# One projection unit in every head step of an attention and spline-FFN kernel: v0 in head 10, v3 in the next batch's head 1, later output, query and key units

## The chip, the cores and the metric

One core of a Trainium2 chip. The metric is the device time of one execution in microseconds, and the before figure is the median of three runs. A profiled execution of the same kernel gives the trace. The engines are named as in the trace: PE (TensorE, the matmuls), PEld (its weight loads), DVE (VectorE), ACT (ScalarE), POOL (GpSimd), and SP (SyncE, which only issues DMAs here).

## What is computed

Four batches of 512 tokens with 512 features, all in float32. After a layer norm, the result is `x + attention(xn) + ffn(xn)`.

```
xn = layernorm(x)
q, k, v = xn@Wq+bq, xn@Wk+bk, xn@Wv+bv          # 16 heads of 32
scores = q k^T / sqrt(32) + slope[h] * distance, causal
ctx = softmax(scores) @ v
attention = ctx @ Wo + bo
ffn: gate, up, down weights (2048 x 512) are Catmull-Rom splines through few control points;
     silu(xn@gate^T) * (xn@up^T) @ down
out = x + attention + ffn
```

To keep float32 precision on fast matmuls, an operand is split into a high part and a low part (high = the value rounded, low = value minus high), and a product is three matmuls: high x high, high x low, low x high.

## The kernel before

The attention of all four batches runs first, then the FFN. The change touches the attention alone. It is a software pipeline of 64 head steps (4 batches x 16 heads), written out by hand and the same on every engine. There is one `step(b, s, ...)` function per engine, and each engine runs its instructions strictly in the order written. What crosses engines goes by semaphores.

In head step s the stages belong to different heads. PE makes the scores of head s (four row tiles of 128 queries, `scores`, L624), transposes the probabilities of head s-2 (`turn_probs`, L638), and multiplies by the values for head s-3 (`weigh_values`, L655 and L658). DVE adds the bias and takes the row maximum of head s (`bias_and_max`, L830, one call for tiles 0 and 1 and one for tiles 2 and 3), copies half of what PE turned (`take_turned`, L839), and normalizes head s-3 (`normalize`, L848, L849, L856). ACT takes exponentials (L1049), rounds them to the high half (`probs_high`, L1057, which waits for PE's last turn of the step, so that it runs at the start of the next step), and copies the remaining turned tile (L1064). POOL makes the low half of the probabilities of head s-1 (`probs_low`, L1160).

There are two score banks. Tile 2 of a head can be scored only when DVE has read tile 0. And `bias_and_max` of head s waits in its first instruction until `probs_low` of head s-2 is done, because the probabilities have two buffers:

```
if (later(b) or s >= 2) and tiles[0] == 0:
    dve.wait_ge(lo_ready, H * b + s - 1)
```

Between these stages the projections are spread over the heads. A unit is 12 matmuls of 512 columns (L583, L584, L585): ("q", c) and ("k", c) make four heads' queries or keys, ("v", t) the values of one tile of 128 tokens, ("o", t) one tile of the output projection of the batch before. `UNITS` says which unit stands in which head step, `TURNS` where a context chunk ("c") or a tile of the next batch's normalized x ("x") is transposed on PE (L668, L573), and `place` says to which batch an entry belongs. The first unit of a step is cut up and put between the attention stages (pieces 0 and 1 ahead of the scores of tiles 2 and 3, piece 2 between the turns, piece 3 behind the values); another unit of the step stands at the end of it. Before, heads 9 and 10 hold no unit, and heads 11 and 13 hold two.

A q or k unit goes on through ACT (`qk_high`, L1023 and L1030), POOL (`qk_low`, L1155), and three DMAs by SP into `q_stack` or `k_stack`. A v unit goes through DVE (`v_take`, L806), and then twice, for heads 0 to 7 and 8 to 15, through ACT (`v_high`, L1042) and DVE (`v_split`, L816, L818, L820, which `SPLITS` places at the end of DVE's step). An x tile goes through statistics (`norm_stats`, L777 to L784), `inverse_std` on POOL (L1148), `norm_apply` on DVE (L789), the transposes, `x_high` on ACT (L1011) and `x_low` on DVE (L798). The units and turns share three PSUM banks in turn, each of which is freed by the low-half operation three entries before. `project_qk` of q0 waits until `x_low` of the last x tile is done.

SP's queue holds the stack DMAs, the store of each sum tile (`store_sum`), the load of the next x tile into the same place (`room_for_x`), and in the last batch the loads for the FFN. Of these, `load_basis` brings the moment basis, for which PE waits in head 12 of the last batch (L695).

Of the kernel before, what the change touches and what calls it, by code (L numbers as in the profile page):

```python
# [239 lines left out]
def build_kernel(nc, x, wq, wk, wv, wo, bq, bk, bv, bo, cpts, c_factor, c_bases, c_mask, c_dist, c_ident, c_scale,  # L240
# [11 lines left out]
    with ExitStack() as outer:  # L252
# [155 lines left out]
        def _(sp):  # L408
# [6 lines left out]
UNITS = {0: [("k", 1)], 1: [("q", 2)], 2: [("o", 0)], 3: [("k", 2)], 4: [("o", 1)], 5: [("o", 2)], 6: [("o", 3)],  # L415
         7: [("q", 3)], 8: [("k", 3)], 11: [("v", 0), ("q", 0)], 12: [("k", 0)], 13: [("v", 1), ("q", 1)],
         14: [("v", 2)], 15: [("v", 3)]}
# [5 lines left out]
SPLITS = {13: [(0, 0)], 14: [(0, 1)], 1: [(0, 2)], 2: [(0, 3)], 4: [(1, 0)], 5: [(1, 1)], 6: [(1, 2)], 7: [(1, 3)]}  # L423
# [23 lines left out]
PJ_FIRST = [("x", t) for t in range(QT)] + [("q", 0), ("k", 0)] + [("v", t) for t in range(QT)] + [("q", 1)] + (  # L447
# [50 lines left out]
def attention(nc, ctx, sems, psum, w_room, v_room, xt_room, stored, lay_out, weights, bq, bk, bv,  # L498
# [65 lines left out]
    def attention_tensor(pe):  # L564
# [144 lines left out]
        def step(b, s, carry):  # L709
# [4 lines left out]
            early, rest = ([], units) if s == 3 else (units[:1], units[1:])  # L714
# [36 lines left out]
        for t in range(QT):  # L751
            project_v(0, t)
# [20 lines left out]
    def attention_vector(dve):  # L773
        def norm_stats(b, tiles):
            for t in tiles:
                dve.wait_ge(x_ld[t], 16 * b + 16)
                dve.bn_stats(stats[:, t, :], x_in[:, t, :]).then_inc(ln_stats, 1)  # L777
# [95 lines left out]
        def step(b, s, carry, carried):  # L873
# [41 lines left out]
            for of, (kind, n) in turns if s not in (3, 11) else []:  # L915
# [29 lines left out]
        norm_stats(0, (0, 1))  # L945
        norm_stats(0, (2, 3))
# [20 lines left out]
        for t in range(QT):  # L967
# [12 lines left out]
        for s in range(HALF, H + 3):  # L980
            step(B - 1, s, False, False)
# [23 lines left out]
    def attention_scalar(act):  # L1005
# [771 lines left out]
```

## Time and profile before

| | |
|---|---|
| time before, median of 3 runs (lowest to highest) | 768.01 us (766.4 to 770.3) |
| the profiled execution's own time | 770.39 us |
| its span, first to last instruction | 768.6 us |
| mean granted TensorE clock, share of full | 0.961 |
| PE busy | 682.4 us (89%) |
| DVE, ACT, POOL busy | 461.0, 445.1, 330.8 us |

A time in the trace counts from the span's start. Head 0 of batch 0 starts at 38.75 us. One round of 16 head steps (head 9 of batch 1 to head 8 of batch 2) goes from 196.63 to 302.56 us. The last heads end near 464 us, and the rest is the FFN. A row of the timeline gives start and length in microseconds, then the engine and the line; in square brackets stands how long the engine was idle before it and what ended that. In a row of the windows, (x56) counts instructions; the three numbers at the end are the granted clock as a share of full speed, the share of the DMA engines, and GB/s.

### The profile page before, as it was taken

What the parts mean: (1) busy time and instruction counts of PE and PEld (TensorE: products, weight loads), DVE (VectorE), ACT (ScalarE), POOL (GpSimd) and SP (SyncE); (2) the same over time, 40 slices, a digit from 0 to 9 for tenths busy, and PEclk for the clock granted to TensorE, in tenths of its full rate; (3) what the DMA queues carried; (4) which work ended last, traced back from release to release, by engine and by line L of the source; (5) the groups of instructions that cost most, each with busy time, mean ns of one, the idle gap of its engine ahead of it and who ended that gap; (6) DMA issues with size and microseconds to landing.
All of it is one profiled execution on the core that took longest, in us unless ns stands there. A gap on an engine that the chain in (4) does not pass through costs nothing.

```text
span 768.6 us, 13687 instructions
## 1 busy us (share of the span) xinstructions
PE 682.4 (89%) x4884; PEld 545.7 (71%) x4884; DVE 461.0 (60%) x1290; ACT 445.1 (58%) x705; POOL 330.8 (43%) x191
## 2 busy tenths in 40 slices
PE   4878789989799898899897777788979999999997
PEld 3766567877578786788776665566758887887885
DVE  6277976879867879768798696665323213223122
ACT  4388758777777977787879764444423332232331
POOL 1565535454545644454546430222225236235334
PEclk9989989999899999899999999999989999999999
DMA  7887386377675374862946938857157475344001
GB/s 244 160 187 126 42 238 117 63 142 172 88 200 80 47 123 103 194 104 43 209 81 96 372 108 270 258 144 275 55 150 246 139 231 173 90 126 128 34 1 55
DMA packets 53067, 109.75 MB, mean 143 GB/s; under 512 B 6408, under 2 KB 6664, under 8 KB 51464
## 3 DMA queue, kind: packets, MB, share of 16 engines
q1 hardware_dynamic: 51416, 106.46, 56.6%
q10 hardware_dynamic: 1584, 2.43, 1.2%
q8 instruction: 39, 0.64, 0.4%
q14 instruction: 28, 0.23, 0.1%
HBM read 59.32 MB, written 25.17 MB: 110 GB/s over the span
## 4 chain that ended last, share of the span: by engine, by line
PE 40%; DVE 5%; issue 4%; POOL 3%; ACT 3%; DMA 2%; ACTq 1%; SPq 0%; POOLq 0%; DVEq 0%
PE bank L1486 6%; PE bank L1488 6%; PE bank L1487 6%; PE bank L1473 3%; PE bank L1474 3%; PE bank L583 3%; PE bank L638 2%; PE bank L585 2%; PE bank L584 2%; POOL resid L1640 2%; DMA bm_early<-bases_scratch 2%; PE bank L624 2%; DVE w_new L1584 1%; ACTq L365 1%; PE bank L655 1%
## 5 line engine op out<-in xcount | busy, mean ns | idle before, releaser
L1160 POOL TENSOR_TENSOR work<-work 128x1280 f16<-128x1280 f32 x64 | 171.3, 2676 | 176.4 <-ACT work L1057 176.4
L1632 POOL TENSOR_TENSOR in_lo<-inner,in_hi 128x512 fp32r<-128x512 f32 x64 | 84.9, 1328 | 201.1 <-ACT in_hi L1550 201.1
L830 DVE CUSTOM_DVE_ANT_0 work<-bank,dist 128x128 f32<-128x128 f32 (+3 forms) x256 | 115.4, 487 | 72.0 <-PE bank L624 48.4
L1049 ACT ACTIVATE work<-work,neg_max 128x128 f32<-128x128 f32 (+3 forms) x256 | 130.0, 561 | 13.8 <-DVE neg_max L830 13.5
L1550 ACT CAST in_hi<-inner 128x512 fp32r<-128x512 f32 x64 | 39.7, 621 | 147.3 <-PE bank L1488 141.3
L1596 DVE TENSOR_TENSOR inner<-bank,silu 128x512 f32<-128x512 f32 x64 | 44.1, 689 | 132.2 <-ACT silu L1544 125.4
L1057 ACT CAST work<-work 128x1280 f16<-128x1280 f32 x64 | 80.6, 1259 | 61.1 <-PE bank L638 60.9
L638 PE MATMUL bank<-ident,work 128*128 128x128 f16 x1280 | 107.7, 229 | 9.1 <-DVE work L839 7.1
L638 PEld LDWEIGHTS bank<-ident,work 128*128 128x128 f16 x1280 | 77.5, 102 | 45.4 <-issue 32.3
L1486 PE MATMUL bank<-w_room,in_hi 128*128 128x512 f32 x256 | 101.6, 397 | 0.4 <-POOL in_lo L1632 0.4
L1487 PE MATMUL bank<-w_room,in_hi 128*128 128x512 f32 x256 | 101.0, 394 | 0.0
L1488 PE MATMUL bank<-w_room,in_lo 128*128 128x512 f32 x256 | 100.9, 394 | 0.0
L624 PE MATMUL bank<-k_stack,q_stack 96*128 96x256 f32 (+2 forms) x256 | 78.1, 380 | 20.3 <-DVE neg_max L830 18.2
L839 DVE COPY work<-bank 128x256 f16<-128x256 f16 (+2 forms) x192 | 75.6, 418 | 6.4 <-PE bank L638 6.2
L624 PEld LDWEIGHTS bank<-k_stack,q_stack 96*128 96x128 f32 x256 | 46.9, 201 | 35.8 <-DVE neg_max L830 29.6
L655 PE MATMUL bank<-v_parts,work 128*128 128x98 bf16 x640 | 68.9, 215 | 2.5 <-issue 2.0
L658 PE MATMUL bank<-v_parts,work 128*128 128x66 bf16 x640 | 66.3, 199 | 0.0
L1064 ACT COPY work<-bank 128x1024 f16<-128x1024 f16 x64 | 64.3, 1005 | 2.5 <-PE bank L638 2.5
L1473 PE MATMUL bank<-z,wgu_hi 128*128 128x512 f32 x128 | 52.1, 407 | 9.2 <-issue 4.8
L655 PEld LDWEIGHTS bank<-v_parts,work 128*128 128x128 f16 x640 | 54.4, 102 | 6.5 <-issue 2.8
L1486 PEld LDWEIGHTS bank<-w_room,in_hi 128*128 128x128 f32 x256 | 49.2, 192 | 11.9 <-POOL in_lo L1632 1.5
L583 PE MATMUL bank<-xt_room,w_room 128*128 128x512 f32 x128 | 55.9, 437 | 1.9 <-DVE xt_room L798 1.9
(100 smaller groups left out, 1298.7 us busy)
## 6 DMA issues: line engine op xcount, KB each, us to landing
q_stack<-parts SPq DMA_DIRECT2D x48, 256.0 KB, 5.7
k_stack<-parts SPq DMA_DIRECT2D x48, 256.0 KB, 6.1
z<-xt_scratch SPq DMA_DIRECT2D x128, 88.0 KB
x_in<-x SPq DMA_DIRECT2D x32, 256.0 KB, 4.0
xt_scratch<-xt_room SPq DMA_DIRECT2D x8, 1024.0 KB, 7.3
xt_room<-xt_scratch SPq DMA_DIRECT2D x6, 1024.0 KB, 10.2
factor<-c_basis SPq DMA_DIRECT2D x5, 1024.0 KB, 9.2
taps<-windows SPq DMA_DIRECT2D x5, 1024.0 KB, 11.1
```

Of the source, the lines that this page charges most:

```text
L583: pe.matmul(bank[:, :], l_hi, r_hi, start=(k == 0), stop=False)
L624: pe.matmul(score_bank[i % 2][:, 0:n], q_stack[:, c % 2, h, i * P:(i + 1) * P], k_stack[:, c % 2, h, 0:n], start=True, stop=True).then_inc ...
L638: mm = pe.transpose(pt_bank[i % 2][:, (part * n + k) * P:(part * n + k + 1) * P], probs16[:, s % 2, part, OFF[i] + k * P:OFF[i] + (k + 1) ...
L655: pe.matmul(bank[:, i * VALUES:(i + 1) * VALUES], probs_t[:, s % 2, at:at + P], v_parts[:, k, s, :], start=(k == 0), stop=False)
L830: dve.tensor_tensor_reduce(probs[:, s % 2, OFF[i]:OFF[i] + n], score_bank[i % 2][:, 0:n], dist[:, S - n:S], -slope(s), 3.4e38, ALU.add, AL ...
L1049: e = act.activation(tile, tile, ACT.Exp, bias=neg_max[:, s % 2, i:i + 1], scale=-1.0)
L1057: act.copy(probs16[:, s % 2, 0, :], probs[:, s % 2, :]).then_inc(hi_ready, 1)
L1160: pool.tensor_tensor(probs16[:, s % 2, 1, :], probs[:, s % 2, :], probs16[:, s % 2, 0, :], ALU.subtract).then_inc(lo_ready, 1)
L1486: pe.matmul(sum_bank[i][:, :], hi, wd_hi[:, g, :], start=(g == 0), stop=False)
L1487: pe.matmul(sum_bank[i][:, :], hi, wd_lo[:, g, :], start=False, stop=False)
L1488: mm = pe.matmul(sum_bank[i][:, :], lo, wd_hi[:, g, :], start=False, stop=(g == NG - 1))
L1632: pool.tensor_tensor(in_lo[k % 2][:, :], inner[:, k % 2, :], in_hi[:, k % 2, :].bitcast(F32), ALU.subtract).then_inc(il_ready, 1)
```

## The change

Each head step now holds exactly one unit. v0 stands in head 10 and v3 in head 1 of the batch that it belongs to (in batch 0 too, where it left the stretch ahead of head 0). q2 and k2 move from heads 1 and 3 to 3 and 4, o1 to o3 from 4, 5, 6 to 5, 6, 7, q3 and k3 from 7 and 8 to 8 and 9, q1 from 13 to 14, v2 from 14 to 15. In head 10 the unit stands at the end of PE's step. On DVE, the low halves of x tiles 0 and 1 stand between the two calls of `bias_and_max` in head 10, `v_take` of v0 stands there in head 11 ahead of the low halves of x tiles 2 and 3, and the statistics of tile 3 with the aggregation of tiles 2 and 3 move from head 8 to head 9. On POOL, `inverse_std` of the second pair moves to step 10, and in every step `qk_low` now stands ahead of `probs_low`. On ACT, `v_high` of v3 stands between the exponentials and `probs_high` of head 2. On SP, each x tile's load is asked for behind the next tile's store, and `load_basis` stands ahead of the stacking of q3 and k3 of the last batch.

```diff
-UNITS = {0: [("k", 1)], 1: [("q", 2)], 2: [("o", 0)], 3: [("k", 2)], 4: [("o", 1)], 5: [("o", 2)], 6: [("o", 3)],
-         7: [("q", 3)], 8: [("k", 3)], 11: [("v", 0), ("q", 0)], 12: [("k", 0)], 13: [("v", 1), ("q", 1)],
-         14: [("v", 2)], 15: [("v", 3)]}
+UNITS = {0: [("k", 1)], 1: [("v", 3)], 2: [("o", 0)], 3: [("q", 2)], 4: [("k", 2)], 5: [("o", 1)], 6: [("o", 2)],
+         7: [("o", 3)], 8: [("q", 3)], 9: [("k", 3)], 10: [("v", 0)], 11: [("q", 0)], 12: [("k", 0)], 13: [("v", 1)],
+         14: [("q", 1)], 15: [("v", 2)]}
-SPLITS = {13: [(0, 0)], 14: [(0, 1)], 1: [(0, 2)], 2: [(0, 3)], 4: [(1, 0)], 5: [(1, 1)], 6: [(1, 2)], 7: [(1, 3)]}
+SPLITS = {13: [(0, 0)], 15: [(0, 1)], 1: [(0, 2)], 2: [(0, 3)], 4: [(1, 0)], 5: [(1, 1)], 6: [(1, 2)], 7: [(1, 3)]}
...
@@ PE, step
-            early, rest = ([], units) if s == 3 else (units[:1], units[1:])
+            early, rest = ([], units) if s in (3, 10) else (units[:1], units[1:])
...
@@ DVE, step
-                if kind == "v" and n > 0:
+                if kind == "v":
                     v_take(of, n)
...
-            if s == 11:
+            if s in (10, 11):
                 for of, (_, n) in turns:
                     x_low(of, n)
...
             if s == HALF - 1 and b < B - 1:
-                norm_stats(b + 1, (0, 1))
+                tile_stats(b + 1, 0)
+                tile_stats(b + 1, 1)
+                pair_stats(b + 1, (0, 1))
             if carry and s == HALF:
-                norm_stats(b + 1, (2, 3))
-            if carry and s == 11:
-                v_take(b + 1, 0)
+                tile_stats(b + 1, 2)
+            if carry and s == HALF + 1:
+                tile_stats(b + 1, 3)
+                pair_stats(b + 1, (2, 3))
...
@@ ACT, step
                 exponentials(b, s)
+                if s == 2:
+                    v_high(b, 0, 3)
                 probs_high(b, s)
...
@@ POOL, step
-            if carry and s in (8, 9):
-                inverse_std(b + 1, s - 8)
-            if halved:
-                probs_low(*halved)
-
+            if carry and s == 8:
+                inverse_std(b + 1, 0)
+            if carry and s == 10:
+                inverse_std(b + 1, 1)
             if s < H and (s or later(b)):
                 for key in active(UNITS, (s - 1) % H, carried):
                     if key[0] in "qk":
                         qk_low(b + place(key, s - 1), *key)
+            if halved:
+                probs_low(*halved)
...
@@ SP
-            store_sum(b - 1, 1)
-            store_sum(b - 1, 2)
-            room_for_x(b, 0)
-            room_for_x(b, 1)
-            store_sum(b - 1, 3)
-            room_for_x(b, 2)
-            room_for_x(b, 3)
+            for q in range(1, QT):
+                store_sum(b - 1, q)
+                room_for_x(b, q - 1)
+            room_for_x(b, QT - 1)
+        load_basis(sp)
         stack(B - 1, 3)
 
         sp.wait_ge(pj_full, pj_total(("k", KC - 1), B - 1))
         load_chunk(sp, 1)
-        load_basis(sp)
```

## Rows read from the trace of the kernel before

**Rows 1.** The page: span; each engine's busy time, share of span, instructions.
```profile
span 768.6 us, 13687 instructions
PE 682.4 (89%) x4884; PEld 545.7 (71%) x4884; DVE 461.0 (60%) x1290; ACT 445.1 (58%) x705; POOL 330.8 (43%) x191
```
**Rows 2.** Windows, a head each (9 to 13, 2, 8): busy, granted clock, DMA.
```profile
196.63:205.96 9.33, 6.01 (x56) 5.16 (x54) 7.58 (x23) 7.77 (x11) 5.72 (x4) 0.72 0.71 108
205.96:212.86 6.90, 4.88 (x54) 4.01 (x53) 5.64 (x18) 5.47 (x9) 2.63 (x2) 0.88 1.03 160
212.86:221.70 8.84, 8.84 (x76) 7.12 (x74) 5.76 (x18) 5.20 (x9) 3.03 (x2) 1.00 0.86 294
221.70:227.29 5.59, 5.59 (x59) 4.45 (x58) 3.49 (x14) 3.80 (x7) 2.33 (x2) 1.00 0.35 70
227.29:235.75 8.46, 8.46 (x73) 6.79 (x70) 6.08 (x19) 7.61 (x11) 5.11 (x3) 1.00 0.67 93
...
258.49:264.65 6.16, 5.62 (x61) 4.44 (x59) 5.41 (x20) 5.98 (x11) 3.87 (x2) 1.00 0.88 123
...
295.63:302.56 6.93, 6.04 (x60) 4.46 (x58) 6.26 (x22) 5.70 (x9) 4.76 (x3) 1.00 0.13 38
sum 105.93, PE 97.54 PEld 78.17 DVE 84.20 ACT 82.47 POOL 53.79; mean PE 6.10 PEld 4.89 DVE 5.26 ACT 5.15 POOL 3.36
```
**Rows 3.** Timeline in head 2, PE and VectorE: start, length (us), line.
```profile
258.49 0.48 PE L624 MATMUL bank<-k_stack,q_stack 96*128 96x256 f32 x2
...
260.06 0.28 DVE L830 CUSTOM_DVE_ANT_0 work<-bank,dist 128x128 f32<-128x128 f32 x1
...
261.18 0.48 PE L583 MATMUL bank<-w_room,ctx_t 128*128 128x512 f32 x1
```
**Rows 4.** Timeline of ScalarE in head 13.
```profile
227.57 1.26 ACT L1057 CAST work<-work 128x1280 f16<-128x1280 f32 x1 [1.44 <-PE bank L638]
...
229.65 0.69 ACT L1023 ACTIVATE qk_full<-bank,b_qk 128x512 f32<-128x512 f32 x1
230.22 0.69 ACT L1030 ACTIVATE parts<-bank,b_qk 128x512 fp32r<-128x512 f32 x1
```
**Rows 5.** Timeline of GpSimd in head 13.
```profile
228.91 2.63 POOL L1160 TENSOR_TENSOR work<-work 128x1280 f16<-128x1280 f32 x1 [4.56 <-ACT work L1057]
231.50 1.28 POOL L1155 TENSOR_TENSOR parts<-qk_full,parts 128x512 fp32r<-128x512 f32 x1
```
**Rows 6.** Timeline of VectorE at the end of head 13.
```profile
232.20 0.73 DVE L856 TENSOR_TENSOR ctx_sb<-ctx_tmp,inv_sum 128x128 f32<-128x128 f32 x1
232.86 0.55 DVE L839 COPY work<-bank 128x768 f16<-128x768 f16 x1
```
**Rows 7.** Timeline in head 9 of batch 0, VectorE and GpSimd.
```profile
95.47 3.33 DVE L789 TENSOR_SCALAR x_in<-x_in,meanvar,rstd 128x512 f32<-128x512 f32 x2
...
95.91 2.61 POOL L1160 TENSOR_TENSOR work<-work 128x1280 f16<-128x1280 f32 x1 [0.99 <-ACT work L1057]
```
**Rows 8.** Timeline of VectorE in head 8: a value split, then the bias.
```profile
297.24 0.42 DVE L816 TENSOR_TENSOR v_room<-v_room,v_parts 128x256 f32<-128x256 f32 x1
...
298.36 0.28 DVE L830 CUSTOM_DVE_ANT_0 work<-bank,dist 128x128 f32<-128x128 f32 x1
```
**Rows 9.** Timeline in head 9 of batch 1, VectorE and PE.
```profile
202.52 0.29 DVE L856 TENSOR_TENSOR ctx_sb<-ctx_tmp,inv_sum 128x128 f32<-128x128 f32 x1
...
204.37 1.94 PE L573 MATMUL bank<-ident,x_in 128*128 128x128 f32 x8 [1.01 <-DVE x_in L789]
```
**Rows 10.** Timeline of VectorE in head 11 of batch 1.
```profile
213.36 0.29 DVE L830 CUSTOM_DVE_ANT_0 work<-bank,dist 128x128 f32<-128x128 f32 x1 [0.37 <-issue]
...
213.92 1.28 DVE L798 TENSOR_TENSOR xt_room<-bank,xt_room 128x512 fp32r<-128x512 f32 x2
```
**Rows 11.** Timeline in head 12 of the last batch, PE.
```profile
431.53 0.47 PE L695 MATMUL bank<-xt_room,bm_early 128*128 128x512 f32 x1 [3.42 <-DMA bm_early<-bases_scratch]
```
**Rows 12.** Timeline at the start of head 0, batch 0, PE.
```profile
38.75 0.48 PE L624 MATMUL bank<-k_stack,q_stack 96*128 96x256 f32 x2 [1.13 <-DMA k_stack<-parts]
```

More of the change, by code:

```diff
@@ L444 @@
 STACK = 16 * ROLES
-PJ_FIRST = [("x", t) for t in range(QT)] + [("q", 0), ("k", 0)] + [("v", t) for t in range(QT)] + [("q", 1)] + (
+PJ_FIRST = [("x", t) for t in range(QT)] + [("q", 0), ("k", 0)] + [("v", t) for t in range(3)] + [("q", 1)] + (
     steps_keys(range(HALF), before=False))
@@ L455 @@
 MOMENTS = {12: 0, 13: 1, 14: 2}
-PJ_LAST = [("k", 3), ("c", 1), ("m", 0), ("m", 1), ("m", 2), ("c", 2), ("o", 0), ("o", 1), ("c", 3), ("o", 2), ("o", 3)]
-PJ_LAST_ENDS = [("k", 3), ("c", 1), ("m", 0), ("m", 1), ("m", 2), ("c", 2), ("c", 3)] + [("o", t) for t in range(QT)]
-CARRIED = [("k", 3)] + [("c", c) for c in range(1, KC)] + [("o", t) for t in range(QT)] + [
+PJ_LAST = [("q", 3), ("k", 3), ("c", 1), ("m", 0), ("m", 1), ("m", 2), ("c", 2), ("o", 0), ("o", 1), ("c", 3), ("o", 2), ("o", 3)]
+PJ_LAST_ENDS = [("q", 3), ("k", 3), ("c", 1), ("m", 0), ("m", 1), ("m", 2), ("c", 2), ("c", 3)] + [("o", t) for t in range(QT)]
+CARRIED = [("q", 3), ("k", 3)] + [("c", c) for c in range(1, KC)] + [("o", t) for t in range(QT)] + [
     ("m", m) for m in range(3)]
@@ L750, in attention_tensor @@
         project_qk(0, "k", 0)
-        for t in range(QT):
+        for t in range(3):
             project_v(0, t)
@@ L773, in attention_vector, with tile_stats, pair_stats @@
     def attention_vector(dve):
[L774 to L777, printed above, removed]
+        def tile_stats(b, t):
+            dve.wait_ge(x_ld[t], 16 * b + 16)
+            dve.bn_stats(stats[:, t, :], x_in[:, t, :]).then_inc(ln_stats, 1)
+        def pair_stats(b, tiles):
             dve.wait_ge(ln_stats, QT * b + tiles[-1] + 1)
@@ L914, in step @@
                 norm_apply(b + 1, 3)
-            for of, (kind, n) in turns if s not in (3, 11) else []:
+            for of, (kind, n) in turns if s not in (3, 10, 11) else []:
                 (x_low if kind == "x" else ctx_low)(of, n)
@@ L944, in attention_vector @@
         dve.memset(minus_half[:], -0.5).then_inc(small_set, 1)
-        norm_stats(0, (0, 1))
-        norm_stats(0, (2, 3))
+        for n in range(2):
+            for t in (2 * n, 2 * n + 1):
+                tile_stats(0, t)
+            pair_stats(0, (2 * n, 2 * n + 1))
         for t in range(QT):
@@ L966, in attention_vector @@
         dve.wait_ge(dist_ld, 16)
-        for t in range(QT):
+        for t in range(3):
             v_take(0, t)
@@ L974, in attention_vector @@
             for s in range(HALF, H):
-                step(b - 1, s, True, s > HALF)
+                step(b - 1, s, True, s > HALF or b > 1)
             for s in range(HALF):
@@ L980, in attention_vector @@
         for s in range(HALF, H + 3):
-            step(B - 1, s, False, False)
+            step(B - 1, s, False, s == HALF)
             if s - 1 in MOMENTS:
@@ L1085, in step @@
             for half, t in SPLITS.get((s + 1) % H, []) if s < H else []:
-                if s >= HALF - 1 and carry and half == 0:
-                    v_high(b + 1, half, t)
-                elif s < HALF - 1:
+                if s >= HALF - 1 and half == 0:
+                    if carry:
+                        v_high(b + 1, half, t)
+                elif s < HALF - 1 and (half, t) != (0, 3):
                     v_high(b, half, t)
```

## Prediction

> **What bounds the kernel now.** I read the page first: PE is busy 89% of the span, the others 43% to 60% [rows 1]. Then I cut one round of 16 head steps into its heads with the windows view. A head with one unit takes 5.59 us and PE is busy for all of it; a head with two takes 8.84 (11, with a context turn) or 8.46 (13). So a unit is worth 8.46 - 5.59 = 2.87 us of PE, and a context turn 8.84 - 8.46 = 0.38. PE idles in few heads: 9 (9.33 us long, 6.01 busy), 10 (6.90, 4.88), 8 (6.93, 6.04) and 2 (6.16, 5.62) [rows 2]. The granted clock is 1.00 nearly everywhere and 0.72 and 0.88 in heads 9 and 10, so part of their time is at the lower level, 1.2 GHz. The round is 105.93 us with 97.54 of PE. The plan's promise is plain: move the two second units into the two empty heads.
>
> Last I read the timeline for the slack of the other engines, counting from a head's start. The first bias of a head has a due time. In head 2 it starts at 260.06, +1.57, and PE resumes its unit at 261.18, 1.12 later [rows 3]; the head is 6.16 - 5.59 = 0.57 long over, of which the context turn is 0.38, so 0.19 is from lateness. In head 8 it starts at 298.36, +2.73 [rows 8], and the head is 1.34 over [rows 2]. Both give the same due time, about +1.39: each microsecond of a later bias is one of the head.
>
> **The change, part by part.**
>
> *POOL's new order.* In head 13 (start 227.29), which handles the k unit of head 12, ACT makes `probs_high` from +0.28 and the unit's high half until 230.91, +3.62 [rows 4]. POOL makes `probs_low` at +1.62 (2.63 us) and `qk_low` after it (1.28 us) [rows 5]. With `qk_low` first, in-order POOL waits for +3.62, so `qk_low` ends at +4.90 and `probs_low` at +7.53, not +4.25. Behind it waits the first bias of the next head (the `lo_ready` wait): 7.53 - 5.59 = +1.94, which is 0.55 late. That is the least price of a q or k unit in a full-length step.
>
> *The collision on top.* DVE's L856 takes 0.29 us alone [rows 9] but 0.73 when it starts at +4.91 in `qk_low`'s span (+4.21 to +5.49); it ends at +5.64, 0.15 after POOL [rows 5, 6]. In batch 0 the two L789 took 3.33 us together where the first `probs_low` of 2.61 lay over them [rows 7]; so POOL's long operation holds them too. In the new order `probs_low` lies at +4.90 to +7.53, just over L856 and the value split that follows L839 (L839 ends at 233.41, +6.12 [rows 6]; the split takes 298.36 - 297.24 = 1.12 [rows 8] and reads two SBUF tensors like L856). The bounds for a split behind a k unit: it isn't held, the bias is due to `probs_low` alone (0.55 late), or it starts only when POOL ends, and the bias starts at 7.53 + 1.12 = 8.65, +3.06 in the next head, 1.67 late (about 1.8 if L856 gets in first and pushes POOL back by part of its 0.29). If the head itself is already d late, L856 falls inside `probs_low` and waits as well: 7.53 + 0.29 + 0.55 + 1.12 = 9.49, which is 2.51 - d late. I take the held case, since L856 is nearest in kind.
>
> The Trainium skill ("SBUF — State Buffer", section "SBUF: two separate sides") says that VectorE and GpSimd take their common port pair as an exclusive lock for the whole instruction, whoever starts first. That L856 ends 0.15 after POOL's operation agrees. By that rule the close race at +4.90 against +4.91 goes to whoever is first; were it always POOL, heads 0 and 2 would pay some 0.7 more each, 4 us over three rounds.
>
> Price for a round: head 13 (q0; no split in 12) 0.85, which is 0.55 plus L856's 0.3; head 14 (k0; 13 already late) 2.51 - 0.85 = 1.66; head 0 (q1; head 15 has a context turn, 0.38 of slack) 1.4; head 2 (k1) 1.8, less the 0.19 it pays today, plus 0.3 for `v_take` of v3 in DVE's chain to the context turn, 1.9; head 5 (q2 comes at the end of 3, so POOL is free early) 0.4; head 6 (k2) 2.51 - 0.4 = 2.1. Sum 8.3 us.
>
> *Heads 9 to 11.* Head 9: POOL holds `probs_low` until about +7.8, so `norm_apply` of the first tile waits; two of these at 0.5 and the last x turn at 0.6 give 9.4 (before 9.33, for other reasons). Head 10: the bias waits for the moved statistics (+0.6), the low halves of x0 and x1 in front of the second bias call take 1.28 [rows 10] more, DVE's copies reach PE's last turns at about +3.9, and v0 stands whole behind them: 3.9 + 0.8 + 2.87 + two x turns of 0.4 = 8.4 (before 6.90). Head 11: q0 is now the early unit and waits for the last `x_low`. DVE starts the bias at 213.36, +0.50, and would be ready for other work at 213.92, +1.06 [rows 10]; `v_take` now goes first (0.6, like one of the two L798), then 1.28: +2.95. The unit before started near +0.55, so head 11 is 5.59 + 2.4 + 0.38 = 8.4 (before 8.84). Together 26.2 against 25.07: +1.1. If ACT's extra k unit ahead of `x_high` binds, heads 9 and 10 trade the wait but the sum stays (7.6 + 9.4).
>
> *Gains.* Head 13 gives back one unit, -2.87. Head 3 is 0.2 longer, from the bias behind a split that starts later. A round: -2.87 + 8.3 + 1.1 + 0.2 = +6.7 us.
>
> *The rest.* Three such rounds: +20.1. In the first one the 3.33 us pair [rows 7] probably falls elsewhere: about -3. Ahead of head 0, v3's leaving gains nothing, because PE waits there for a stack DMA that it doesn't touch [rows 12]. Heads 0 to 7 of batch 0 keep four units, but pay two held splits: 2 x 1.7 = +3.4. In the last batch `load_basis` early takes away the wait of 3.42 us [rows 11]; against it k3 goes to head 9, which had none (up to 2.87), and POOL's order costs 0.55 or more once: about 0. SP's other new order puts the load of x tile 2 behind the store of tile 3, which I cost at nothing, because the stores come a head later anyway and the statistics of tile 3 moved by a head; without that cover DVE's statistics in head 7 or 8 wait, at most some 3 us in one batch. Sum: 20.1 - 3 + 3.4 + 0 = +20.5.
>
> The profiled execution has a span of 768.6 and a time of 770.39 us, 2.4 above the median. Its sum would be 789 (span). On the median: 768.0 + 20.5 = 788.5, so **788.5 us**.
>
> **Rivals.**
>
> *(1) POOL's operation doesn't hold the split; only `lo_ready` binds.* For it: splits have hardly lain under `probs_low` so far. Against: L856 and L789 are held. Price a round: heads 13, 2 and 6 pay 0.55, head 0 0.2, `v_take` 0.3, and head 9 shrinks to 7.6 with head 10 at 9.4: 25.3 - 25.07 = +0.2. Sum: 2.15 + 0.2 + 0.2 - 2.87 = -0.3. With +1 for batch 0: about 769.
>
> *(2) The other side: POOL's lateness costs nothing.* If ACT reaches the k and q units some half microsecond earlier than in rows 4 (its exponentials have slack where PE is late), `probs_low` ends by +6.98 = 5.59 + 1.39 and nothing waits: it decides from there. Then a round is -2.87 + 0.2 + 0.2 = -2.5, three are -7.4, and the 3.42 of the last batch comes as well: 757.
>
> *(3) The empty heads fill up entirely.* x's chain hides behind PE, heads 9 to 11 are 6.4 + 6.4 + 6.0 = 18.8 instead of 25.07: another -6.3 a round, 740. Against: q0's wait for `x_low` is in the code, and DVE's rows give +2.95.
>
> *(4) As my forecast, but the clock falls more often.* The new waits of 1.4 to 2.4 us stand in six heads. The granted clock was 0.72 in head 9, where PE was busy 6.01 of 9.33 us [rows 2]. One more low stretch a round with a unit in it costs up to 2.87: 797.
>
> **How the numbers follow.** Forecast 0.52, rival 1 0.18, rival 2 0.14, rival 3 0.04, rival 4 0.12. The forecast's own range is 780 to 796 (each of six prices by a third, the race for 4 us). The range of 758 to 800 leaves out rival 3, the lower half of 2 and the upper part of 4, 0.2 or a little less. A difference within 0.5% (3.8 us) is about what a measurement of this kernel can't tell from none. Slower by more: forecast, 4, and a little of 1, 0.66. Within: most of 1, 0.12. Faster: 2, 3 and the rest of 1, 0.22.
>
> **What the profile after would show.** Heads 2, 6, 14 and 0 longer than 7 us, with L830 preceded by L816 to L820 that start as L1160 ends, and L1155 ahead of L1160. Head 13 near 6.5, not 5.6. In head 11 an idle PE of about 2 us ended by DVE L798. Head 10 over 8 us. No wait on `bm_early`. The prediction is wrong if the first bias in the heads after a q or k unit still starts by +1.4, or if L816 runs at 0.41 us inside L1160.

## The result and the profile after

The changed kernel takes 846.0 us in the median of four runs (843.5 to 847.47), against 768.18 us (766.4 to 770.3) for the kernel before beside it. The ratio is 1.1003, with a 95% interval of 1.0966 to 1.104. The forecast of 788.5 us had the sign, and its range of 758 to 800 missed the size: the loss is 78 us and not 20. The profiled execution took 846.91 us.

The page of the changed kernel, its span and the busy time of each engine:

```profile
span 845.1 us, 13687 instructions
PE 709.4 (84%) x4884; PEld 560.9 (66%) x4884; DVE 529.5 (63%) x1290; ACT 447.3 (53%) x705; POOL 331.3 (39%) x191
```

The instruction counts are those of before [rows 1]. PE is busy 27 us longer with the same matmuls. Most of that is the clock: an estimate from the means of 0.936 and 0.961 over the two spans, at half speed where it is low, gives 24 us. DVE is busy 68.5 us longer with the same instructions, which is waiting inside an instruction: 43 us of it are in the three instructions of the value split, 18 in L857 (L856 before), and 4 in `norm_apply`. ACT and POOL have hardly changed. Where the time lies, by windows of the changed kernel: heads 0 to 8 of batch 0, and the first two of the three rounds of 16 heads. The table has the other stretches too.

```profile
38.40:99.67 61.27, 45.21 (x361) 36.38 (x361) 48.39 (x141) 39.64 (x63) 25.77 (x12) 0.79 0.50 96
99.67:225.61 125.94, 104.18 (x932) 80.98 (x930) 102.92 (x279) 83.10 (x128) 54.38 (x26) 0.93 0.53 116
225.61:354.90 129.29, 106.35 (x933) 82.38 (x930) 105.87 (x279) 83.02 (x128) 54.05 (x26) 0.92 0.48 90
```

| stretch, us | before | after | difference | forecast |
|---|---|---|---|---|
| heads 0 to 8, batch 0 | 48.91 | 61.27 | +12.4 | +3.4 |
| round 1 | 108.97 | 125.94 | +17.0 | +3.7 |
| round 2 | 105.93 | 129.29 | +23.4 | +6.7 |
| round 3 | 106.49 | 129.46 | +23.0 | +6.7 |
| last half batch | 41.95 | 45.28 | +3.3 | 0 |
| FFN and the stretch ahead of head 0 | 356.4 | 353.9 | -2.5 | 0 |

In round 2 PE is idle for 129.29 - 106.35 = 22.9 us, before for 105.93 - 97.54 = 8.4 [rows 2]. So 14.5 us of the 23.4 are idle time, and 106.35 - 97.54 = 8.8 are the same matmuls taking longer. About 7 of these 8.8 are the clock, by an estimate from the means: 129.29 us at 0.92 hold about 21 us of the low level (twice 0.08 of the time), heads 9 and 10 of before [rows 2] about 7, and each such microsecond costs half of one. The rest shows at full clock too: head 13 has 6.02 us of PE at 1.00. The same view for heads of that round (11, 13 and 14 of batch 1; 0, 2 and 6 of batch 2), and first for head 0 of the round before:

```profile
155.82:165.11 9.29, 6.05 (x60) 4.46 (x58) 9.01 (x18) 4.79 (x7) 4.55 (x2) 1.00 0.60 86
...
244.34:254.43 10.09, 7.72 (x64) 5.86 (x61) 5.72 (x17) 2.85 (x6) 0.00 (x0) 0.83 0.87 304
...
260.03:267.12 7.09, 6.02 (x60) 4.45 (x58) 6.64 (x16) 5.58 (x10) 5.16 (x3) 1.00 0.93 137
267.12:277.34 10.22, 7.64 (x61) 5.60 (x58) 8.45 (x20) 4.36 (x6) 3.10 (x2) 0.83 0.51 61
...
283.34:294.19 10.85, 7.61 (x59) 5.73 (x58) 9.09 (x18) 4.79 (x7) 4.56 (x2) 0.84 0.53 74
...
299.81:310.67 10.86, 7.33 (x61) 5.68 (x59) 9.79 (x20) 4.96 (x9) 4.84 (x2) 0.84 0.53 73
...
330.37:341.36 10.99, 7.60 (x60) 5.53 (x58) 9.24 (x20) 4.66 (x7) 4.24 (x2) 0.84 0.67 119
```

Four heads carry most of it: 14, 0, 2 and 6, with 10.2 to 11.0 us each. The prediction named these four, because in each the first bias stands behind a value split and a late `probs_low`. It gave them 7.2, 7.0, 8.1 and 7.7 us. In each of them DVE is busy 8.4 to 9.8 us. Here is why: the timeline of the changed kernel, VectorE, then GpSimd and PE, at the end of head 1 and the start of head 2 (299.81) of batch 2.

```profile
299.59 0.56 DVE L840 COPY work<-bank 128x768 f16<-128x768 f16 x1 [0.17 <-PE bank L638]
300.06 2.13 DVE L817 TENSOR_TENSOR v_room<-v_room,v_parts 128x256 f32<-128x256 f32 x1
302.23 2.58 DVE L819 CAST v_parts<-v_room 128x256 bf16<-128x256 f32 x1
304.84 0.42 DVE L821 TENSOR_TENSOR v_parts<-v_room,v_parts 128x256 bf16<-128x256 f32 x1
305.18 0.28 DVE L831 CUSTOM_DVE_ANT_0 work<-bank,dist 128x128 f32<-128x128 f32 x1
...
299.14 5.51 POOL L1169 TENSOR_TENSOR work<-work 128x1280 f16<-128x1280 f32 x2
...
305.53 0.85 PE L624 MATMUL bank<-k_stack,q_stack 96*128 96x384 f32 x2 [3.54 <-DVE neg_max L831]
```

POOL's two `probs_low`, that of head 0 and that of head 1, run back to back from 299.14 to 304.65. The split is three instructions. Its first, L817, is held until the first `probs_low` ends; its second, L819, starts when the second `probs_low` already runs, and is held until that ends too. The third, L821, takes its usual 0.42 us. The copy L840, which reads PSUM, also lies under the first `probs_low` and keeps its time, 0.56 us. The first bias starts at 305.18, +5.37 in the head. The due time read from before was +1.39, so the bias is 3.98 us late: 5.59 + 0.38 for the context turn + 3.98 = 9.95 us. Some 0.9 us remain, which go with the clock, in finer windows of the same head:

```profile
305.53:306.53 1.00, 1.00 (x5) 0.69 (x6) 0.95 (x4) 0.83 (x2) 0.00 (x0) 1.00 0.17 18
306.53:309.90 3.37, 3.37 (x30) 2.75 (x30) 2.42 (x9) 1.63 (x3) 0.00 (x0) 0.50 0.01 2
```

PE idles for 3.5 us; about 1 us after it has resumed, the granted clock falls from 2.4 to 1.2 GHz, and is back at the end of the head. Each of the heads 11, 14, 0, 2 and 6 of round 2 shows a mean of 0.83 or 0.84. Of the heads before, 9 and 10 were below 1.00 [rows 2]. What the clock alone costs can be read from head 0. Its bias starts at +5.08 in each of the three rounds, 3.69 late, which makes 5.59 + 3.69 = 9.28 us. In round 1 the clock stayed at 1.00 and the head took 9.29; in round 2 it fell and the head took 10.85. So both the due time and a price of 1.6 us for such a low stretch come out of the trace.

Head 0 is held like head 2: L817 takes 2.22 us and L819 2.58. In heads 6 and 14 two `probs_low` hold DVE as well, but the first of them meets L857, ahead of the split. VectorE at the end of head 5 and in head 6 (330.37) of batch 2 with both `probs_low`, then VectorE and GpSimd in head 14 (267.12) of batch 1:

```profile
329.68 2.45 DVE L857 TENSOR_TENSOR ctx_sb<-ctx_tmp,inv_sum 128x128 f32<-128x128 f32 x1
...
332.53 2.36 DVE L817 TENSOR_TENSOR v_room<-v_room,v_parts 128x256 f32<-128x256 f32 x1
...
329.37 5.24 POOL L1169 TENSOR_TENSOR work<-work 128x1280 f16<-128x1280 f32 x2
...
268.92 2.72 DVE L821 TENSOR_TENSOR v_parts<-v_room,v_parts 128x256 bf16<-128x256 f32 x1
...
268.75 2.61 POOL L1169 TENSOR_TENSOR work<-work 128x1280 f16<-128x1280 f32 x1 [1.14 <-ACT work L1063]
```

In head 14 the first `probs_low` holds L857 for 1.32 us, and the second comes 1.14 us after it and meets the third part of the split. So what the four heads share is that DVE's chain of L857 and the split is held by two `probs_low`, not that the split is held twice.

### The profile page after: what moved, and what is told of

It reads as the page before. It is cut to its first block, busy times and chain, and to the rows that moved or that the text cites. A ratio compares the mean times of both kernels' runs of the same rounds, so it can differ in the third digit from the quotient of the medians.

```text
span 845.1 us, 13687 instructions
## 1 busy us (share of the span) xinstructions
PE 709.4 (84%) x4884; PEld 560.9 (66%) x4884; DVE 529.5 (63%) x1290; ACT 447.3 (53%) x705; POOL 331.3 (39%) x191
## 4 chain that ended last, share of the span: by engine, by line
PE 43%; DVE 13%; issue 5%; POOL 3%; DMA 3%; ACT 3%; ACTq 1%; SPq 1%; POOLq 0%; DVEq 0%
PE bank L1493 5%; PE bank L1495 5%; PE bank L1494 5%; PE bank L638 4%; PE bank L583 4%; PE bank L585 3%; PE bank L624 3%; PE bank L584 3%; PE bank L1480 3%; PE bank L1481 2%; POOL resid L1647 2%; DVE v_room L817 2%; PE bank L655 2%; DVE ctx_sb L857 2%; DVE v_parts L819 2%
## 5 line engine op out<-in xcount | busy, mean ns | idle before, releaser
L1055 ACT ACTIVATE work<-work,neg_max 128x128 f32<-128x128 f32 (+3 forms) x256 | 132.0, 563 | 80.5 <-DVE neg_max L831 80.2
L624 PE MATMUL bank<-k_stack,q_stack 96*128 96x256 f32 (+2 forms) x256 | 83.8, 403 | 71.1 <-DVE neg_max L831 66.7
L638 PE MATMUL bank<-ident,work 128*128 128x128 f16 x1280 | 115.2, 238 | 8.3 <-DVE work L840 6.5
L638 PEld LDWEIGHTS bank<-ident,work 128*128 128x128 f16 x1280 | 82.4, 107 | 51.4 <-issue 38.5
L1164 POOL TENSOR_TENSOR parts<-qk_full,parts 128x512 fp32r<-128x512 f32 x31 | 39.8, 1285 | 184.0 <-ACT parts L1036 184.0
L840 DVE COPY work<-bank 128x256 f16<-128x256 f16 (+2 forms) x192 | 76.9, 418 | 18.8 <-PE bank L638 18.0
L655 PE MATMUL bank<-v_parts,work 128*128 128x98 bf16 x640 | 72.8, 221 | 2.4 <-issue 2.0
L658 PE MATMUL bank<-v_parts,work 128*128 128x66 bf16 x640 | 69.8, 204 | 0.0
L583 PE MATMUL bank<-xt_room,w_room 128*128 128x512 f32 x128 | 61.6, 481 | 8.9 <-DVE xt_room L799 8.9
L655 PEld LDWEIGHTS bank<-v_parts,work 128*128 128x128 f16 x640 | 58.3, 107 | 6.3 <-issue 2.8
```

What stands on the lines that cost most here:

```text
L583: pe.matmul(bank[:, :], l_hi, r_hi, start=(k == 0), stop=False)
L624: pe.matmul(score_bank[i % 2][:, 0:n], q_stack[:, c % 2, h, i * P:(i + 1) * P], k_stack[:, c % 2, h, 0:n], start=True, stop=True).then_inc ...
L638: mm = pe.transpose(pt_bank[i % 2][:, (part * n + k) * P:(part * n + k + 1) * P], probs16[:, s % 2, part, OFF[i] + k * P:OFF[i] + (k + 1) ...
L655: pe.matmul(bank[:, i * VALUES:(i + 1) * VALUES], probs_t[:, s % 2, at:at + P], v_parts[:, k, s, :], start=(k == 0), stop=False)
L1055: e = act.activation(tile, tile, ACT.Exp, bias=neg_max[:, s % 2, i:i + 1], scale=-1.0)
```

## The experiments

All ratios are to the kernel before on the same chip, where it took 769.8 to 770.9 us in the median; kernels e1 to e4 ran together, then e5 to e8, then e9 to e11.

**e1, the changed kernel with POOL's old order.** If the order is the cause, this takes most of the loss back.

```diff
+            if halved:
+                probs_low(*halved)
             if s < H and (s or later(b)):
                 ... qk_low ...
-            if halved:
-                probs_low(*halved)
```

> The changed kernel with one edit undone: on POOL, probs_low stands ahead of qk_low again. Theory A (POOL's order does nearly all of the damage: a value split on DVE lies under POOL's long operations and holds up the next head's first bias): heads 0, 2, 6 and 14 fall back from 10 to 11 us to about 6, head 13 from 7.1 to 5.6, and the time to 755 to 768 us. Theory B (the new places of the units themselves cost most, by heads 9 to 11 and by the clock): the time stays above 820 us.

Measured: 774.77 us (770.87 to 778.74), ratio 1.0062 (1.0029 to 1.0095). Some 71 of the 78 us go with this order, as theory A has it, but the time stays above A's 755 to 768. Windows of e1: heads 10 and 11 of batch 2, then head 8 of batch 2.

```profile
313.78:324.64 10.86, 8.44 (x68) 7.04 (x66) 6.22 (x22) 7.03 (x12) 7.14 (x4) 0.84 0.88 114
324.64:334.73 10.09, 7.73 (x63) 5.92 (x62) 5.72 (x17) 3.12 (x7) 0.00 (x0) 0.83 1.01 321
298.26:306.22 7.96, 6.06 (x59) 4.45 (x58) 6.62 (x23) 4.74 (x7) 3.53 (x2) 1.00 0.27 95
```

Head 13 has lost its second unit and is 5.60 us long, and head 14 is back at 5.74. But in round 3 heads 9 to 11 take 7.56 + 10.86 + 10.09 = 28.5 us where they took 25.0, and head 8, at the end of round 2, takes 7.96 for 6.93. So the new places of the units on their own gain nothing: rounds 2 and 3 take 106.16 and 107.09 us for 105.93 and 106.49.

**e2, the kernel before with only POOL's new order.** The same edit in the other direction tells whether the order needs the new places to do harm.

```diff
-            if halved:
-                probs_low(*halved)
-
             if s < H and (s or later(b)):
                 ... qk_low ...
+            if halved:
+                probs_low(*halved)
```

> The kernel before with only POOL's order changed: qk_low ahead of probs_low, all units where they were. Theory A: the splits in heads 1, 2 and 13, which follow a k or q unit, are held; heads 2 and 3 grow by 4 to 5 us each, head 14 by 1 or more, so about 10 us for each of three rounds: 795 to 815 us. Theory B: under 775 us.

Measured: 797.92 us (794.77 to 800.12), ratio 1.0357 (1.0296 to 1.0419): 27 us from one moved call, in the range. Its parts were expected otherwise. In round 2, head 3 grows by 3.8 us, but head 2 by 2.3 only and head 14 by nothing (5.54). Head 9, which the expectation did not name, grows by 3.4, to 12.7; there, in batch 2, the pair of `norm_apply` takes 3.32 us (at 333.09), with a `probs_low` over it from 333.52. That the sum fits is in part luck. Rows of e2: windows of head 3 of batch 2, then the timeline at the end of head 2, VectorE and GpSimd.

```profile
282.63:294.75 12.12, 8.92 (x62) 7.47 (x61) 8.22 (x19) 5.44 (x8) 2.37 (x1) 0.72 0.06 24
...
282.49 2.79 DVE L816 TENSOR_TENSOR v_room<-v_room,v_parts 128x256 f32<-128x256 f32 x1
285.32 0.29 DVE L818 CAST v_parts<-v_room 128x256 bf16<-128x256 f32 x1
...
282.39 2.61 POOL L1160 TENSOR_TENSOR work<-work 128x1280 f16<-128x1280 f32 x1 [0.45 <-ACT work L1057]
```

Here POOL starts 0.10 us ahead of L816 and the split is held once. No other GpSimd instruction follows, and L818 takes its 0.29 us.

**e3, the split held at most once.** The changed kernel, in which POOL, before `probs_low`, waits for the third part of the split that stands ahead of it on DVE. The second hold cannot happen then, and all else stays.

```diff
+                for half, t in SPLITS.get((s - 1) % H, []):
+                    of = halved[0] + (1 if halved[1] >= HALF else 0)
+                    if of < B and not (half == 0 and halved[1] >= HALF and of == B):
+                        pool.wait_ge(v_done, 2 * QT * of + QT * half + t + 1)
                 probs_low(*halved)
```

> The changed kernel, with POOL waiting before probs_low of a head until the value split of that DVE step is done, so that a split can be held by at most one probs_low. Theory C (held twice: the split's first operation waits for one probs_low, its second for the next, which POOL starts back to back): heads 0, 2, 6 and 14 fall from 10 to 11 us to about 7 to 8, and the time to 795 to 815 us. Theory D (held once, as the prediction had it, and the rest is a fallen clock): no change beyond 1%, 838 to 850 us.

Measured: 802.72 us (801.47 to 805.66), ratio 1.0428 (1.0372 to 1.0485). Theory C gave 795 to 815, D 838 to 850. Timeline of e3 at the same place, VectorE and GpSimd:

```profile
275.59 2.13 DVE L817 TENSOR_TENSOR v_room<-v_room,v_parts 128x256 f32<-128x256 f32 x1
277.75 0.29 DVE L819 CAST v_parts<-v_room 128x256 bf16<-128x256 f32 x1
...
278.43 0.28 DVE L831 CUSTOM_DVE_ANT_0 work<-bank,dist 128x128 f32<-128x128 f32 x1
...
274.69 2.74 POOL L1169 TENSOR_TENSOR work<-work 128x1280 f16<-128x1280 f32 x1
278.59 2.64 POOL L1169 TENSOR_TENSOR work<-work 128x1280 f16<-128x1280 f32 x1 [1.15 <-DVE v_parts L821]
```

L817 takes 2.13 us as before it, L819 0.29 instead of 2.58, because POOL starts its second `probs_low` only behind L821, after 1.15 us of idling. The first bias starts at 278.43, +3.09 in the head (275.34), where the forecast had +3.06. Windows of e3: head 6 of batch 1, head 14 of batch 2, head 0 of batch 3, and heads 2 and 6 of batch 2.

```profile
188.10:195.60 7.50, 6.04 (x60) 4.45 (x58) 7.22 (x20) 4.67 (x7) 4.28 (x2) 1.00 1.03 207
...
366.69:373.03 6.34, 6.04 (x60) 4.45 (x58) 6.07 (x20) 4.36 (x6) 3.13 (x2) 1.00 0.75 95
379.05:386.04 6.99, 6.04 (x59) 4.44 (x57) 6.71 (x18) 4.77 (x7) 4.44 (x2) 1.00 0.81 113
275.34:282.83 7.49, 5.92 (x61) 4.45 (x59) 7.32 (x20) 5.40 (x9) 4.74 (x2) 1.00 0.77 106
302.54:311.59 9.05, 7.62 (x60) 5.61 (x58) 7.29 (x20) 4.66 (x7) 4.26 (x2) 0.81 0.84 145
```

At full clock all four now come out at or below the forecast: 6.34, 6.99, 7.49 and 7.50 us for 7.2, 7.0, 8.1 and 7.7. In round 2 head 6 meets a low stretch and takes 9.05, 1.55 more. So e3 takes away the second hold in every one of the four, and with it most of the low stretches behind it.

**e4 to e7, where the new places lose.** e4 is e1 with q0 at the end of head 11. e5 is e1 with x tiles 2 and 3 turned ahead of v0 in head 10. e6 is e5 with ACT's `x_high` ahead of the high half of k3 in head 9. e7 is e6 with SP loading x tile 2 ahead of the store of tile 3, and with POOL's `qk_low` first in the last half batch alone.

```diff
# e4
-            early, rest = ([], units) if s in (3, 10) else (units[:1], units[1:])
+            early, rest = ([], units) if s in (3, 10, 11) else (units[:1], units[1:])
# e5, PE and DVE (x_low of tiles 2 and 3 goes to the end of step 10)
-            for key in rest:
+            for key in rest if s != 10 else []:
...
+            for key in rest if s == 10 else []:
+                unit(b, s, key)
# e6, ACT
-            for key in active(UNITS, s, carry):
+            for key in active(UNITS, s, carry) if s != 9 else []:
...
+            for key in active(UNITS, s, carry) if s == 9 else []:
+                qk_high(b + place(key, s), *key)
# e7, SP
             room_for_x(b, 0)
             room_for_x(b, 1)
+            room_for_x(b, 2)
             store_sum(b - 1, 3)
-            room_for_x(b, 2)
             room_for_x(b, 3)
# e7, POOL
+            halved_first = not (b == B - 1 and s > HALF)
+            if halved and halved_first:
+                probs_low(*halved)
             ... qk_low ...
+            if halved and not halved_first:
+                probs_low(*halved)
```

> As the run with probs_low first, and in addition q0 in head 11 stands whole at the end of PE's step and not cut up ahead of the scores of tiles 2 and 3. If the wait of q0 for the last x_low is PE's loss in head 11 (8.5 to 10.1 us there), it shrinks by 1 to 2 us in each of three rounds: 3 to 6 us less than the run with probs_low first alone. If the wait is only moved, no difference.

> On top of the run with probs_low first: in head 10 PE turns x tiles 2 and 3 ahead of v0 and not behind it, and DVE makes their low halves at the end of head 10, under v0. Theory E (q0's wait in head 11 for the last x_low is a real loss of 2.4 us a round, and it brings the lower clock with it): head 11 falls from 8.5 to 10.1 us to 6.0, head 10 stays within 9.5 to 10.9, and the time is 6 to 12 us under that run, 762 to 769. Theory F (the wait is only moved): 772 to 777 us.

> As e5, and in head 9 ACT makes the high halves of x ahead of those of k3, so that DVE's x_low in head 10, with the second bias call behind it, need not wait for k3. Head 10 shrinks by about 1.2 us in three rounds: 3 to 4 us less than e5. If ACT is not what DVE waits for there, no difference.

> As e6, and SP stores two sum tiles before it loads x tiles, with the load of tile 2 ahead of the store of tile 3, and POOL makes qk_low first in the last half batch alone, where no value split follows. Head 8 loses its wait for x_in (9.2 and 8.0 us in two rounds, 6.9 before): 2 to 3 us; head 12 of the last batch waits 2.6 us less for k_stack. Together 3 to 5 us less than e6.

Measured: 774.45, 773.52, 776.42 and 778.02 us, ratios 1.005 (1.0021 to 1.008), 1.0056 (1.0023 to 1.0089), 1.0084 (1.0051 to 1.0118) and 1.0102 (1.0073 to 1.0131). None beats e1 beyond the intervals, and none of the expected gains came. e5 did mend head 11, 5.93 us for 10.09, but head 10 grew to 11.5 to 13.2, and in e6 to 15.2. In e7 head 8 kept its length, 9.5 and 9.3 us in rounds 1 and 2, so this order of SP did not shorten it. Rows of e6 in head 10 of batch 1: the window, then VectorE's `norm_apply`, GpSimd's `probs_low` and PE.

```profile
207.46:222.68 15.22, 10.02 (x68) 7.89 (x67) 10.20 (x24) 7.82 (x13) 7.12 (x4) 0.78 0.93 159
...
213.21 3.33 DVE L793 TENSOR_SCALAR x_in<-x_in,meanvar,rstd 128x512 f32<-128x512 f32 x2
...
213.64 2.62 POOL L1176 TENSOR_TENSOR work<-work 128x1280 f16<-128x1280 f32 x1 [0.97 <-ACT work L1068]
...
216.69 1.09 PE L574 MATMUL bank<-ident,x_in 128*128 128x128 f32 x4 [2.17 <-DVE x_in L793]
```

The next `probs_low` starts 0.43 us after the first `norm_apply`; the second meets it, and the pair takes 3.33 us, as in [rows 7]. PE waits 2.17 us for the second tile, and the mean clock of the head is 0.78. So moving x's chain up had put it under another GpSimd instruction.

**e8, the changed kernel without the value split.** Its second and third parts of the values are left out: L817 and L821 are memsets of zero, L819 a nop. It tells what POOL's lateness costs if DVE's split is not there to be held.

```diff
-            dve.tensor_tensor(full, full, first, ALU.subtract).then_inc(v_rest, 1)
+            dve.memset(second, 0.0).then_inc(v_rest, 1)
...
-            dve.tensor_copy(second, full).then_inc(v_mid, 1)
+            dve.nop(nofuse=True).then_inc(v_mid, 1)
...
-            dve.tensor_tensor(third, full, second, ALU.subtract).then_inc(v_done, 1)
+            dve.memset(third, 0.0).then_inc(v_done, 1)
```

> The changed kernel without the value split's three operations on two SBUF operands: the second and third part of the values are set to zero in their place (this leaves out part of the computation, and POOL's new order stays). What is left is the wait of the bias for a late probs_low. If only the hold of the split matters: heads 0, 2, 6 and 14 within 0.1 us of 5.6 to 6.2, and the time 770 to 780 us. If the late probs_low costs as the prediction has it (0.55 us a head, with the held L857 and norm_apply left in): heads 2, 6, 13 and 14 at 6.1 to 6.9, and 780 to 800 us.

Measured: 780.27 us (778.85 to 782.5), ratio 1.0137 (1.0105 to 1.017), at the border of the two theories. Windows of e8, heads 0, 2 and 6 of batch 2:

```profile
253.87:260.08 6.21, 6.06 (x59) 4.46 (x58) 4.26 (x17) 4.62 (x7) 4.41 (x2) 1.00 0.94 129
265.68:272.36 6.68, 5.92 (x61) 4.44 (x59) 4.95 (x19) 5.40 (x9) 4.69 (x2) 1.00 0.86 119
291.24:297.74 6.50, 6.05 (x60) 4.46 (x58) 4.65 (x18) 4.66 (x8) 4.70 (x2) 1.00 0.97 134
```

They are 0.6, 0.5 and 0.9 us longer than before. The first bias stands idle for 1.4 to 1.5 us ahead of its start at +1.99, +2.27 and +2.28: this is the price of `lo_ready` alone, which the forecast had as 0.55 with the bias at +1.94. Head 14 grows by 0.2 only (5.76), below the expected 6.1, and head 13 takes 7.11, since L857 is still held there. The four kernels now make a chain for round 2: 129.29 us changed; 116.7 held at most once (e3); 109.4 with no split to hold (e8, which also saves the split's own 1.1 us a head); 106.2 with the old order (e1).

**e9, the new places with the port kept apart.** e7 with three further edits: POOL waits for `norm_apply` before `probs_low` in steps 10 and 11, the value split of head 7 stands ahead of the statistics, and SP's order is the changed kernel's.

```diff
+            if carry and s in (10, 11):
+                pool.wait_ge(xn_ready, QT * (b + 1) + 2 * (s - 9))
```

> The new units, with POOL's probs_low first again except in the last half batch, and everything else placed so that no DVE two-port operation of the x chain meets a POOL operation: x tiles 2 and 3 turned ahead of v0 in head 10, x_high ahead of qk_high in head 9, POOL waiting for norm_apply before probs_low in steps 10 and 11, in head 7 the value split ahead of the statistics. Theory G (what is left of the new units' loss is the held norm_apply and the late x chain): head 10 goes from 15 to about 10 us and head 8 from 9.3 to about 7, which by three rounds gives 755 to 765 us. Rival H (the heads 9 to 11 are bound by TensorE's work and the low clock whatever the order): 772 us or more.

Windows of e9, heads 8 to 10 of batch 1, then VectorE and GpSimd in head 10:

```profile
185.53:192.54 7.01, 6.06 (x60) 4.45 (x57) 6.59 (x23) 4.74 (x7) 3.29 (x2) 1.00 0.24 70
192.54:200.25 7.71, 6.96 (x69) 5.30 (x66) 7.01 (x20) 6.82 (x10) 3.89 (x2) 1.00 0.35 95
200.25:210.36 10.11, 7.08 (x68) 5.76 (x65) 7.85 (x24) 7.85 (x13) 7.15 (x4) 1.00 0.86 115
...
205.99 0.99 DVE L793 TENSOR_SCALAR x_in<-x_in,meanvar,rstd 128x512 f32<-128x512 f32 x2
...
207.06 2.64 POOL L1176 TENSOR_TENSOR work<-work 128x1280 f16<-128x1280 f32 x1 [1.61 <-DVE x_in L793]
```

The heads do what theory G said: the pair of `norm_apply` takes 0.99 us instead of 3.33, head 10 is 10.1, head 8 is 7.0, and head 11 keeps the 5.93 of e5. The first two rounds take 101.83 and 102.02 us for 108.97 and 105.93 before, with a clock of 1.00. But the time is 768.04 us (761.34 to 773.34), ratio 0.9962 (0.9926 to 0.9999), which is between the two expectations. Heads 0 to 8 of batch 0 cost 52.4 us for 48.9, the last half batch 43.8 for 41.95, and in round 3 of the profiled execution a low stretch makes head 10 12.9 us long. This execution took 761.44; others were up to 12 us longer. SP's order is the changed kernel's again, and still head 8 is short; which of e9's other edits did that, its run does not tell apart.

**e10 and e11, two parts for the kernel before.** e10 issues only the load of the basis earlier. e11 is e10 with e9's wait on POOL.

```diff
# e10, SP
+        load_basis(sp)
         stack(B - 1, 3)
...
         load_chunk(sp, 1)
-        load_basis(sp)
# e11, POOL, further
+            if carry and s in (10, 11):
+                pool.wait_ge(xn_ready, QT * (b + 1) + 2 * (s - 9))
```

> The kernel before, with only the load of the basis for the last batch issued ahead of the stack of the batch's last keys. If the wait for the basis in head 12 of the last batch is a loss of its own, the kernel gains what that wait is, about 3.4 us (764 to 767 us where the kernel before shows 768 to 770). If the wait only moves to the next transfer behind it, no difference (within 0.5 per cent).

> The same as e10, and POOL waits for norm_apply before probs_low in steps 10 and 11. If the norm_apply that POOL holds in head 9 of batch 0 is what makes that head 12.0 us there against 9.3 in the others, the head goes to about 9.4 and the kernel gains 2.5 us more than in e10 (761 to 764 us). If probs_low coming later costs as much as the hold, no difference to e10.

e10: 764.75 us (761.3 to 768.36), ratio 0.9939 (0.9917 to 0.9962). Head 12 of the last batch in its windows:

```profile
422.76:428.57 5.81, 5.37 (x56) 4.32 (x55) 5.33 (x18) 5.78 (x9) 2.70 (x2) 1.00 1.01 416
```

It was 10.06 us, with the wait of [rows 11], and the last half batch is 37.29 us for 41.95. The expected gain was 3.4 us; 0.61% is 4.7, and the expected 764 to 767 us hold. e11: 765.19 us (760.18 to 770.17), ratio 0.9947 (0.992 to 0.9974), no difference to e10 and above the expected 761 to 764. Its head 9 of batch 0 is 9.3 us as expected, against 12.03 before. But that head is 9.34 us in e10's trace too, without the wait: the collision of [rows 7] is a close race that this execution of e10 did not lose. How often the kernel before loses it was not measured, so e11's theory stays open. These are the fastest kernels of the study.

## Why the direction was right and the size wrong

**The failed step is "The collision on top", in its case "it starts only when POOL ends".** The prediction took the value split as one block of 1.12 us, and let L856 and the split wait for the end of one and the same `probs_low`. That put the bias at +3.06 where nothing else is late. The trace shows a chain of short instructions with a fresh contest before each, and a GpSimd that, being late itself, has its next `probs_low` ready at once (heads 0, 2 and 6) or 1.14 us later (head 14). The chain is held by both, and the bias starts at +5.37 in head 2, and at +5.08, +5.22 and +4.44 in heads 0, 6 and 14. The prediction had the means to see it: [rows 8] give the split's first instruction alone as 0.42 us, and `probs_high` of the next head is ready at +1.54 [rows 4], before a POOL that runs until +1.94 is free. It asked what comes late behind POOL's instruction, but not what POOL does next. e3 measures this step: without the second hold the bias of head 2 starts at +3.09, the four heads take what the forecast gave them or less, and the time falls by 43 us to 802.72, close above the forecast's range. The low clock stretches that the second hold brought are in these 43.

**The clock, the forecast's rival 4, came on top.** It was priced as one more low stretch a round. Before, rounds 2 and 3 have one each, in heads 9 and 10. The changed kernel has four in round 1 and six in each of the others, and the same matmuls take 8.8 us more in round 2. PE waits for 2.3 to 3.5 us eighteen times in the three rounds; sixteen of these waits have a low stretch at their end or up to 1.4 us behind it. Two have none, in head 11 of batch 0 (2.36 us) and head 0 of batch 1 (3.24 us), so such a wait makes the fall likely and not certain here. The mean clock is 0.933 to 0.938 in the changed kernel's executions, 0.949 to 0.965 in e3's and 0.961 in the profile before. Holding of the split and clock together are e8's difference, some 66 of 78 us, which includes the split's own time.

**Right in kind and size:** the price of `lo_ready` alone (0.55 forecast, 0.5 to 0.9 in e8); the held case in kind, and with one hold in size (e3); heads 5 (5.95 for 6.0) and 9 (9.1 for 9.4). Head 3 was to grow by 0.2 and did not (8.24 us for 8.28). In head 11 the forecast idle PE of about 2 us shows in the timeline of the changed kernel:

```profile
247.42 0.47 PE L583 MATMUL bank<-xt_room,w_room 128*128 128x512 f32 x1 [2.37 <-DVE xt_room L799]
```

**Right in kind, mis-sized:** head 11 was 10.1 and not 8.4 in rounds 2 and 3, because that wait also brought a low stretch; in round 1, with the same wait at a clock of 1.00, it was 8.54, as forecast. Head 10 was 8.3, 9.6 and 9.9 for 8.4. Head 13 was 7.1 and not 6.44: the race of [rows 5, 6] was lost. The timeline of the changed kernel at the end of head 12, VectorE and GpSimd:

```profile
259.35 2.60 DVE L857 TENSOR_TENSOR ctx_sb<-ctx_tmp,inv_sum 128x128 f32<-128x128 f32 x1
...
259.17 2.64 POOL L1169 TENSOR_TENSOR work<-work 128x1280 f16<-128x1280 f32 x1
```

POOL starts 0.18 us ahead, and L857 takes 2.60 us instead of 0.29. The Trainium skill ("SBUF — State Buffer", section "SBUF: two separate sides") says that the port pair which VectorE and GpSimd share is given whole to whoever starts first, for the whole instruction, and the rows here agree: a held instruction ends 0.1 to 0.3 us after the GpSimd instruction that holds it. By that rule each instruction contends on its own; the prediction had cited it for one race and had not applied it to the three of the split.

**Batch 0 and the end.** Heads 0 to 8 of batch 0 were forecast at +3.4, two held splits, and measured +12.4. The chains of heads 2 and 6 are held twice there too (+3.7 and +6.3), with the clock at 0.79. Another 2.4 us are head 0. The prediction had v3's leaving the stretch ahead of it gain nothing, "because PE waits there for a stack DMA". It cost: that wait is now 3.85 us and not 1.13 [rows 12], the clock falls, and head 0 takes 5.92 us at 0.55 for 3.48. Head 0 takes 4.8 us or more in every kernel with v3 moved, and 3.5 in every one without (e2, e10, e11). Of the 3.33 us pair of [rows 7] 2.6 us are left, since the first `norm_apply` is held for 2.17 us; head 9 is 9.2 us long and not 12.0. In the last batch the wait for the basis went, as forecast, and the late k3 took more than it: +3.3 for "about 0". e10 shows that the early load alone is worth 4.7 us, so the moved units and POOL's order cost some 8 there. In e1 that shows as the wait of head 12's first scores, 4.94 us until 433.76. SP issues the last of k3's three stack DMAs at 425.90, and the longest of the `k_stack` transfers there takes 7.8 us to land, which is 433.7: the scores wait for k3.

**Of the rivals,** 1 and 2 fell with the first trace. Rival 3, the empty heads fill up entirely, was right about the reserve and wrong about this kernel: e9's heads 9 to 11 take 23.8 us for 25.07, where 18.8 was the bound. In rival 1's price the three heads add up to 25.4 and not 25.3, and its time to 768 rather than 769; neither changes the argument.

## What to carry to other kernels

When an engine that shares a port comes late, read what it does next as well: its next instruction may already be ready, and a sequence of short instructions on the other engine can then lose the port more than once. Price such a sequence instruction by instruction, and check in the trace that every long GpSimd instruction lies over VectorE work that reads PSUM (the copy L840 kept its 0.56 us), or over nothing; one semaphore wait on the engine with slack keeps them apart (e3, e9). A wait of over 2 us in the middle of dense matmuls should be priced with the low clock stretch that came with sixteen of the eighteen here, about 1.6 us each in heads 0, 6 and 11, and a moved unit with the transfers and chains that it carries behind it, not by its own 2.87 us.

## What was not expected of the hardware

- Two GpSimd instructions back to back left no place between them for more than one waiting VectorE instruction: L817 ended 0.3 us after the first, L819 was then held for the rest of the second (2.13 and 2.58 us for 0.42 and 0.29 alone).
- The prediction's reason for the hold was that the split "reads two SBUF tensors". The cast L819 reads one tensor and is held too, as `norm_apply` is: 0.53 us alone, and 2.88 at most in heads 9 and 10 of batch 1 of the changed kernel.
- The low clock came with sixteen of eighteen waits of 2.3 to 3.5 us. In round 2 its estimated 7 us are almost a third of the loss of 23.4. e9 has no wait of 2 us or more left in its rounds. The first two ran at 1.00; in the third the clock fell all the same, where PE had waited 1.1 and then 1.7 us.
